# Where a pair of matmul operand buffers lies in SBUF: moved from a 512-byte line's start to 64 bytes ahead of one

## The reference

```python
def ffn(x):                       # w1, w2: 1024x256, h1, h2: 1024x1024, w3: 256x1024, entries -1, 0, 1
    h = silu(tlin(x, w1, s1)) * tlin(x, w2, s2)
    h = gelu(tlin(h, h1, t1))     # first square layer
    h = gelu(tlin(h, h2, t2))     # second square layer
    return tlin(h, w3, s3)        # tlin(x, w, s) = (x @ w.T) * s
x = x + 0.5 * ffn(layernorm(x))
x = x + (gelu(irfft(rfft(layernorm(x)) * rfft(K))[:L]) @ W.T + b)   # K from the S4D parameters
x = x + 0.5 * ffn(layernorm(x))
```

## Time and the profile before

| | |
|---|---|
| median of 3 runs | 1422.92 us (1422.16 to 1424.48) |
| span of the profiled execution, first to last instruction | 1420.9 us |
| outside the span, against the median | 2.0 us |
| TensorE busy, share of the span | 1415.5 us, 100% |
| VectorE busy | 986.1 us, 69% |
| ScalarE busy | 478.9 us, 34% |
| mean granted TensorE clock | 1.000 |

### The profile page before, as it was taken

How to read it: one execution, slowest core, us unless ns; L and a number is a source line. 1 busy time by engine, 2 the same in 40 slices (tenths; PEclk the granted TensorE clock), 3 DMA queues, 4 the chain that set the end, 5 groups by cost and what they waited for, 6 DMA issues and landing times.

```text
span 1420.9 us, 17300 instructions
## 1 busy us (share of the span) xinstructions
PE 1415.5 (100%) x6923; PEld 1164.5 (82%) x6923; DVE 986.1 (69%) x1742; ACT 478.9 (34%) x724; POOL 48.8 (3%) x43
## 2 busy tenths in 40 slices
PE   9999999999999999999999999999999999999999
PEld 4888888888878888788787888878878788888887
DVE  7877778675878888758888577784777755354433
ACT  5524342523425124232232332422424223141321
POOL 0000000000000000010000100001000010000000
PEclk9999999999999999999999999999999999999999
DMA  9001000012023111131210312112120112010000
GB/s 365 23 5 40 16 30 30 19 42 67 35 76 145 49 58 60 42 104 60 75 60 12 134 45 74 43 33 100 60 74 15 60 41 74 1 45 0 30 1 16
DMA packets 54434, 80.28 MB, mean 56 GB/s; under 512 B 2768, under 2 KB 46160, under 8 KB 53072
## 3 DMA queue, kind: packets, MB, share of 16 engines
q1 hardware_dynamic: 54352, 79.15, 16.4%
HBM read 57.12 MB, written 22.02 MB: 56 GB/s over the span
## 4 chain that ended last, share of the span: by engine, by line
PE 97%; issue 1%; DMA 1%; DVE 0%; SPq 0%
PE ps L1362 80%; PE ps L1451 8%; PE ps L1502 3%; PE ps L1555 2%; PE ps L1338 1%; PE ps L1434 1%; DMA raws<-in_weights 1%; PE ps L1436 1%; PE ps L1496 1%; PE ps L1497 1%; PE ps L1464 1%; PE ps L1545 0%; PE ps L1479 0%; DVE hid_a_lo L1251 0%; SPq L320 0%
## 5 line engine op out<-in xcount | busy, mean ns | idle before, releaser
L511 ACT ACTIVATE act_o<-ps,scales 128x512 f32<-128x512 f32 x384 | 264.5, 689 | 858.8 <-PE ps L1362 856.8
L1362 PE MATMUL ps<-hid_b_hi,h 128*128 128x512 f32 x1024 | 401.4, 392 | 0.0
L1362 PE MATMUL ps<-hid_b_lo,h 128*128 128x512 f32 x1024 | 398.6, 389 | 0.0
L1362 PE MATMUL ps<-hid_a_hi,h 128*128 128x512 f32 x984 | 386.9, 393 | 0.0
L1362 PE MATMUL ps<-hid_a_lo,h 128*128 128x512 f32 x984 | 383.0, 389 | 0.0
L1362 PEld LDWEIGHTS ps<-hid_b_hi,h 128*128 128x128 f32 x1024 | 192.2, 188 | 41.2 <-issue 1.2
L1362 PEld LDWEIGHTS ps<-hid_b_lo,h 128*128 128x128 f32 x1024 | 192.2, 188 | 40.7 <-issue 1.2
L1362 PEld LDWEIGHTS ps<-hid_a_hi,h 128*128 128x128 f32 x984 | 184.7, 188 | 40.5 <-issue 2.2
L1362 PEld LDWEIGHTS ps<-hid_a_lo,h 128*128 128x128 f32 x984 | 184.7, 188 | 40.2 <-issue 2.2
L1362 PE MATMUL ps<-hid_b_hi,w 128*128 128x512 f32 x480 | 187.2, 390 | 0.0
L1362 PE MATMUL ps<-hid_b_lo,w 128*128 128x512 f32 x480 | 186.8, 389 | 0.0
(11 more groups left out here) (275 smaller groups left out, 1277.6 us busy)
## 6 DMA issues: line engine op xcount, KB each, us to landing
ks<-k_d SPq DMA_DIRECT2D x32, 512.0 KB, 3.8
raws<-in_weights SPq DMA_DIRECT2D x9, 1024.0 KB, 13.7
xin<-in_x SPq DMA_DIRECT2D x8, 512.0 KB, 3.8
x_d<-xin SPq DMA_DIRECT2D x8, 512.0 KB, 2.8
z_d<-xin SPq DMA_DIRECT2D x8, 512.0 KB, 2.8
zb<-z_d SPq DMA_DIRECT2D x8, 512.0 KB, 4.9
wb<-x_d SPq DMA_DIRECT2D x8, 512.0 KB, 4.2
x_d<-wb SPq DMA_DIRECT2D x8, 512.0 KB, 3.5
```

The source lines that it names most:

```text
L511: A(act_o[:, k % ACT_SLOTS], bank(source), func, scale=scale).then_inc(s_act, 1)
L1362: last = MM(o, weight[:, k, cols].bitcast(dt), part[:, k].bitcast(dt), start=(k == 0 and i == 0), stop=(k == n - 1 and i == len(act_) - 1))
```

## The change

The pair `hid_b_hi`, `hid_b_lo` is taken out of its place behind `hid_a` and put ahead of `w3`, where `w3` began. It is 32768 bytes long, a whole number of lines, so it begins 64 bytes ahead of a line, and `w3` behind it does too, as before. `w3`, the small tensors behind it, the four other matrices, and `hid_a` move up by 32768 bytes and keep their place within a line. What lies behind `hid_b` before (`xin`, `act_o`, `gz` and on) stays at its address. `zf` and `low` lie over `hid_b_hi` and go with it. The lists of instructions of all five engines, with their waits, are the same row by row; only addresses differ.

```diff
         scales, small, single, LAST = zone(0, ("scales", [P, 4, KH]), ("small", [P, N_SMALL]), ("single", [P, 4]))
         LAST += (LINE - 64 - base - LAST) % LINE
+        HB = LAST
+        hid_b_hi, hid_b_lo, LAST = zone(HB, ("hid_b_hi", [P, KH, TOK], F32R), ("hid_b_lo", [P, KH, TOK], F32R))
+        assert (base + HB) % LINE == (base + LAST) % LINE == LINE - 64
         w3, FRONT = zone(LAST, ("w3", [P, KH, D], F32R))
         raw_3, _ = zone(LAST, ("raw_3", [P, KH * D]))
         flag, expo, FRONT = zone(FRONT, ("flag", [P, 1], I32), ("expo", [P, J]))
@@ -207,11 +210,9 @@
         assert (base + X0) % LINE == 0
         count, warm, ones = (single[:, i:i + 1] for i in range(3))
 
-        hid_a_hi, hid_a_lo, hid_b_hi, hid_b_lo, xin, act_o, gz, Z0 = zone(
+        hid_a_hi, hid_a_lo, xin, act_o, gz, Z0 = zone(
             X0, ("hid_a_hi", [P, KH, TOK], F32R), ("hid_a_lo", [P, KH, TOK], F32R),
-            ("hid_b_hi", [P, KH, TOK], F32R), ("hid_b_lo", [P, KH, TOK], F32R),
             ("xin", [P, J, D]), ("act_o", [P, ACT_SLOTS, TOK]), ("gz", [P, J, D]))
-        HB = X0 + 2 * 4 * KH * TOK
         zf, low, _ = zone(HB, ("zf", [P, KD, TOK]), ("low", [P, CHUNK], I32))
```

## The result

The changed kernel takes 1442.43 us (median of 4 runs, 1442.31 to 1443.03), the kernel before 1422.84 us beside it. The ratio is 1.0138, with a 95% interval of 1.0123 to 1.0152: 19.6 us slower. I had forecast 1422.8 us within 1418.5 to 1436.0, so the forecast missed, with its range too.

The account below looks back on a forecast made before the run. TensorE, busy for all but 5 us, bounds the kernel: matmul count times pace. Span 1420.9 - 0.1 + 0 = 1420.8 us, plus 2.0 us outside, gives 1422.8 us; range 1418.5 to 1436.0 us.

Parts of the forecast that it names:

- What bounds the kernel, and the price of a nanosecond: TensorE's matmul count times pace sets the time; one nanosecond on each of 3008 `hid_b` matmuls is 3.0 us.
- Writing `hid_b`, and PE's waits: VectorE's cast and subtraction into `hid_b`: cost 0, as even a 693 ns cast stays hidden; uncovered, 4.3 us in all.
- `zf` and `low`: Plain `float32` matmuls on `zf` in tile 0: cost 0, with a sixteenth's surcharge of 1.5 us as bound.
- Reading `hid_b` 64 bytes ahead of a line, at 0: Matmuls with `hid_b` moving keep their pace per column at the new place, judged from `w3`: cost and gain 0.
- The doubt that I had named: In layer three, each matmul's own 128-column load might be the bound, so a faster `w3` would not show.
- The bounds: For reading `hid_b` in 3008 matmuls: at best 37.0 us gained at `float32`'s pace, at worst 12.6 us lost.
- the new place brings the slow pace: Rival: `hid_b` matmuls fall into layer three's slower pace, 4.2 ns each, 12.6 us more, 1435.5 us; chance 0.12.
- The rival that freed the pace: The 64-byte offset separates both operands and removes the `hid_b` matmuls' surcharge: 37.0 us less, 1385.9 us; chance 0.09.
- The other rivals: Layer three loses its fast pace, 3.8 us more, chance 0.05; VectorE's writes become late, up to 1427 us, chance 0.03.
- A reading: Against a slower layer three: the pace settles within three matmuls of each stage's start in any neighbourhood.
- The rule beside the rows: Skill page's matmul issue time, columns over 2.4 GHz plus 2.5 ns: 32.8 us of `hid_b` stages unexplained, 1390.1 us if removed.
- The borders: Stage changes between `w3`, `hid_b` and `hid_a`, with layer three's entry: 0.1 us of gain altogether.

Follow-up runs that it names:

- the second sweep: Matmuls alone, nothing else of the reference computed: `w3` at 13 offsets, narrower loads, 384 and 128 moving columns, plain `float32`; layer three's form took 7.26 to 7.68 us.
- the sweeps: Three programs of matmuls alone, nothing else of the reference computed, varying offsets, column counts and loads; none undercut 226.7 ns for 512 columns.
- the half dose: Against the changed kernel, `hid_b_hi` goes on a line while `hid_b_lo` stays 64 bytes ahead, matrices on a line: 1432.23 us, ratio 1.0063.

## Why the prediction was wrong, point by point

- *What bounds the kernel, and the price of a nanosecond.* Right. Of the 19.6 us, 19.1 came through the pace of the 3008 matmuls that I had counted, 6.4 ns each on average, and the rest through layer three.
- *Writing `hid_b`, and PE's waits.* Right: 426 and 692 ns, no new wait.
- *`zf` and `low`.* Right as to `float32`: no surcharge at 448 in the second sweep (lines 113 and 115).
- *Reading `hid_b` 64 bytes ahead of a line, at 0.* This step failed. It said: "Either place gives the same pace per column", from `w3` at 448 with 0.444 ns a column and operands on a line with 0.443, and took the surcharge for a share of the columns. Both halves are wrong. The surcharge is no share: at equal places it is 13.4 ns for 512 columns, 16.6 for 480, 16.0 for 448, 13.8 for 384, 13.2 for 320 and 13.0 to 13.3 for 256, where a sixteenth would be 6.7. And the two rows differed in two things at once, place and shape; with place alone changed, `w3` goes from 7.27 to 7.68 us on a line, and `hid_b` from 72.55 to 73.82 us off it. Two effects of opposite sign had given the same quotient, and that they met at 0.444 and 0.443 was chance. The doubt that I had named, a layer three bound by its loads, deserved more weight: with 128 moving columns the pace is still 110.8 to 111.6 ns.
- *The bounds.* The lower one, 37 us of gain, never came near. The upper one had the right place and the wrong size: I took the 4.2 ns between layer three's two paces, and it was 6.6 ns at each `hid_b` matmul. 12.6 us became 19.1, and the range ended 6.4 us short of the result. The rival "the new place brings the slow pace", at 0.12, is the one nearest to what came. It looked for the cause in how loads and moving reads fall to each other; the experiments with the matrices moved along show that the difference between the two places is what counts, and no run shows how the reads meet.
- *The rival that freed the pace.* It held that equal places are the cause of the surcharge. For 512 columns they are the best places found. For 256 columns it was right: `w3` takes 7.68 us at equal places and 7.27 apart.
- *The other rivals.* Layer three lost its fast pace in two tiles on balance, 0.5 us, but not by the distance of 32 KB: with the pair ahead and on a line, fifteen of them take 7.27 or 7.28 us and only the last 7.55. VectorE was not late.
- *A reading.* I wrote that the pace settles within three matmuls of a stage's start in any neighbourhood. Between the narrow matmuls of line 1479, the kernel before has 32 matmuls with `hid_b` in 7.47 us (start 245.50), not 32 x 226.7 = 7.25: the first starts are 336, 236, 229, 232 and 231 ns apart, and only then 227.
- *The rule beside the rows.* The Trainium skill, "TensorE: Matmul & The Clock Gate", section "Back-to-back issue gap", has no term for the address. No run here reached its 215.8 ns for 512 columns of `float32r`; the sweeps gave 226.7 to 236.7 by nothing but the places.
- *The borders.* Instead of the 0.1 us of gain, 0.5 us were lost: tiles 0 and 15 gained 0.27 us each, tiles 1, 3, 13 and 14 lost as much each.

Shown: for 512 columns with both parts placed alike, the difference modulo 256 bytes between moving and stationary place sets the pace, and it accounts for the change's cost. Open: whether it is the two read streams meeting in SBUF, why widths of 320 to 480 columns show none of it, and why a stretch can keep either of two paces.

## What to carry to other kernels

A row at the new place is evidence only if its shape is that of the operands to be moved: place and shape acted against each other here. Where `float32r` matmuls fill the time, give moving and stationary operand of a 512-column product the same place modulo 256 bytes, try the 256-column products apart, and read the pace from pieces of the chain, start to start, since the listed durations moved by 1.3 to 1.5% where the pace moved by 2.9%. With PE at 100%, 64 bytes of placement in matmuls that make up 48% of the span were worth 1.4% of the kernel.

## What the runs showed of the hardware that I had not expected

- `float32r` matmuls of 512 columns with a fresh load of 128 take 226.7 ns at a place difference of 0 or 256 bytes, 229.1 at 64, 232.3 to 233.3 at 128, 233.3 at 192, and 236.7 at 4.
- With 320, 384, 448 and 480 columns, differences of 0 and 192 bytes give the same pace within 0.7 ns.
- The best difference depends on the column count: at 256 columns, 0 takes 119.7 to 120 ns and 192 takes 113.6 or 117.8.
- A stretch can run at either of two paces with the same operands, and keeps the one it enters with: 7.27 or 7.54 us for layer three, 226.8 or 236.6 ns for layer one of the half dose.
- Loading fewer stationary columns does not make it faster: 231.4 and 231.7 ns with 32 columns loaded.
- Plain `float32` shows none of it: 27.52 and 27.47 us at the two places.
